# Attention with centred weights: in the first group, the means and the centring of the next group's weights one step later

## The reference

```python
x = x + tanh(g_xattn) * xattn(_layernorm(x), ctx, ...)
x = x + tanh(g_ffn)   * moe(_layernorm(x), ...)
# xattn, 16 query heads, 8 key heads, head size 128
q  = _ln(fp8_linear(ln_out, wq,  q_in_scale));   k = _ln(fp8_linear(ln_out, wk, k_in_scale))
v  = fp8_linear(ln_out, wv, v_in_scale)          # self attention:  core = gqa(q, k, v)
qx = _ln(fp8_linear(ln_out, wqx, qx_in_scale))
kx, vx = split(ctx @ w_kv_x.T); kx = _ln(kx)     # cross attention: xout = gqa(qx, kx, vx)
out = (div_clamp_fp8(cat(core, xout), proj_smooth) @ wproj.T) * scale
# moe: 8 experts, top 2, silu(x @ Wg) * (x @ Wu) @ Wd, weighted sum
# _ln(y) subtracts the mean of each head's 128 outputs and divides by their deviation
```

## Time and profile before

| | |
|---|---|
| median of 3 runs | 1162.47 us |
| the profiled execution: its time, its span | 1163.21 us, 1161.2 us |
| PE busy | 1088.4 us, 94% of the span |
| DVE busy | 816.1 us, 70% |
| ACT busy | 697.0 us, 60% |
| POOL busy | 494.0 us, 43% |
| mean granted TensorE clock | 0.974 |
| DMA, mean over the span | 92 GB/s |

### The profile page before, as it was taken

The page is one execution under the profiler, slowest core; times in us unless marked ns, Lnnn a source line. Parts: engine busy times, 40 slices in busy tenths (PEclk is TensorE's granted clock), DMA queues, the critical chain, the costliest instruction groups (busy, mean ns, idle before and its releaser), DMA issues. The chain is left out here.

```text
span 1161.2 us, 19646 instructions
## 1 busy us (share of the span) xinstructions
PE 1088.4 (94%) x5662; PEld 891.7 (77%) x5662; DVE 816.1 (70%) x1692; ACT 697.0 (60%) x2015; POOL 494.0 (43%) x571
## 2 busy tenths in 40 slices
PE   3499999999999999999999999998999869999996
PEld 2377878888888878888888888886888747777785
DVE  7989997887887797777788777777554785565000
ACT  7557878757887865788876665673231323444332
POOL 4154454445554445444535455452000125565432
PEclk8799999999999999999999999999999879999998
DMA  7231111114111125111112311111954347674220
GB/s 254 68 113 35 35 50 46 45 48 185 44 45 35 35 62 189 35 44 53 39 41 80 115 42 38 43 36 69 336 174 163 127 137 216 176 237 111 51 45 0
DMA packets 52820, 107.40 MB, mean 92 GB/s; under 512 B 6064, under 2 KB 27056, under 8 KB 51184
## 3 DMA queue, kind: packets, MB, share of 16 engines
q1 hardware_dynamic: 48016, 97.00, 25.6%
q0 software_dynamic: 4704, 9.18, 3.5%
HBM read 91.48 MB, written 16.52 MB: 93 GB/s over the span
## 5 line engine op out<-in xcount | busy, mean ns | idle before, releaser
L523 POOL TENSOR_TENSOR rs<-va,mhalf 125x2 f32<-125x2 f32 (+1 forms) x180 | 204.9, 1139 | 14.2 <-POOL va L516 0.2
L529 POOL TENSOR_TENSOR c_lo<-c_raw,c_hi 128x500 fp32r<-128x500 f32 x96 | 125.0, 1303 | 190.2 <-ACT c_hi L581 190.2
L796 PE MATMUL bank<-w_hi,c_hi 128*125 128x512 f32 x384 | 166.0, 432 | 9.9 <-POOL c_lo L529 9.9
L796 PE MATMUL bank<-w_hi,c_lo 128*125 128x512 f32 x384 | 151.8, 395 | 0.0
L796 PE MATMUL bank<-w_lo,c_hi 128*125 128x512 f32 x384 | 151.7, 395 | 0.0
L516 POOL TENSOR_TENSOR va<-ss,epst 125x2 f32<-125x2 f32 (+1 forms) x180 | 48.3, 269 | 199.6 <-DVE ss L1077 121.0
L770 PE MATMUL bank<-w_hi,xqs 128*128 128x512 f32 (+2 forms) x464 | 110.2, 359 | 16.1 <-DVE xqs L1069 10.1
L770 PE MATMUL bank<-w_lo,xqs 128*128 128x512 f32 (+2 forms) x464 | 100.8, 339 | 0.1
L660 ACT ACTIVATE work<-bank,nmax 112x375 f32<-112x375 f32 x128 | 73.6, 585 | 41.9 <-DVE nmax L1106 41.7
L840 PE MATMUL bank<-kxT,qxT 128*112 128x375 f32 x256 | 96.9, 480 | 0.0
L796 PEld LDWEIGHTS bank<-w_hi,c_hi 128*125 128x125 f32 x384 | 71.7, 187 | 28.3 <-issue 10.2
(11 more groups left out here) (265 smaller groups left out, 2813.1 us busy)
## 6 DMA issues: line engine op xcount, KB each, us to landing
c_raw<-in_ctxT SPq DMA_DIRECT2D x96, 250.0 KB, 2.7
shared<-in_w_in SPq DMA_DIRECT2D x13, 1024.0 KB, 8.5
shared<-in_wproj SPq DMA_DIRECT2D x32, 256.0 KB, 4.1
raw_g<-in_Wg SPq DMA_DIRECT2D x8, 1024.0 KB, 6.5
raw_u<-in_Wu SPq DMA_DIRECT2D x8, 1024.0 KB, 6.6
raw_d<-in_Wd SPq DMA_DIRECT2D x8, 1024.0 KB, 5.6
cat_scratch<-results SPq DMA_DIRECT2D x32, 224.0 KB, 2.0
shared<-cat_scratch SPq DMA_DIRECT2D x2, 1792.0 KB, 9.2
```

The source lines that it names most:

```text
L523: pool.tensor_tensor(rs[0:rows, lo:hi], va[0:rows, lo:hi], mhalf[0:rows, lo:hi], ALU.pow).then_inc(rs_done, 1)
L529: pool.tensor_tensor(flat(c_lo[:, k, :, :]), flat(c_raw[:, k, :, :]), flat(c_hi[:, k, :, :]).bitcast(F32), ALU.subtract).then_inc(cl_done, 1)
L796: m = pe.matmul(bank[0:CT, :], a[:, ch, k, :], w[:, k, CKX:CV], start=(i == 0), stop=(i == 3 * KB - 1))
```

## The change

In the first group alone, block k is summed in step k + 2 instead of k + 1 and centred in step k + 3 instead of k + 2. The last block is therefore centred in step (0, 6), which is also the "queries" step; since `w_high(g, 0)` needs all blocks, it is moved there from before `take(s, 4)` to after the last part of the centring. In the other groups nothing changes.

```diff
+def centred_from(gp):
+    return 3 if gp == 0 else 2
@@ passes
-                k = u - 2 if 2 <= u < 2 + KB else None
+                k = u - centred_from(gp) if 0 <= u - centred_from(gp) < KB else None
@@ ACT, step
             if k is not None: weights.centre(act, g, k, 0)
-            if change == "queries": w_high(g, 0, change)
+            if change == "queries" and k is None: w_high(g, 0, change)
             if A: take(s, 4)
             if k is not None: weights.centre(act, g, k, 1)
             if k is not None: weights.centre(act, g, k, 2)
+            if change == "queries" and k is not None: w_high(g, 0, change)
             if change == "queries": w_high(g, 1, change)
@@ DVE, step
-            if change is None and g is not None and s[1] <= KB: weights.means(v, g, s[1] - 1)
+            if g is not None and change is None and 0 <= s[1] + 1 - centred_from(s[0]) < KB:
+                weights.means(v, g, s[1] + 1 - centred_from(s[0]))
```

## The result

The change made the kernel a little slower. Twenty runs each: 1167.23 us median against 1164.02 us, 3.2 us apart; ratio of the changed kernel to the kernel before 1.0031, 95% interval 1.0021 to 1.0042. In time the ratio is +3.6 us, from 2.4 to 4.9. The direction and the mechanism were as forecast; the forecast of +2.4 us was too small, and the windows of the steps tell where. One of the twelve runs of experiment seven, 1844.84 us at a mean granted clock of 0.556, stands apart from all others and is left out of the ratio given there.

The account below looks back on a forecast made before the run. PE was taken to bound group 1 and DVE the first group's steps 2 to 4; -1.4 + 2.8 + 1.0 = +2.4 us on the median 1162.47 gave 1164.9 us, own range 1163.5 to 1166.5, wide range 1160.3 to 1168.3.

Parts of the forecast that it names:

- the net loss: At the step change, (0,6) with (0,7): PE's stall less what it gives back, plus the clock; 2.6 to 4.9 us.
- The gain at (0,2): PE's step (0,2): without the sums DVE is no longer late, so -1.4 us, at the lower end 1.0 gained.
- rival B: Steps (0,2) to (0,5): early start persists, all at 23.83 us; 1161.7 us, or 1157.8 with the stall hidden; chance 0.12.
- ACT's centring in (0,6): ACT's queue: 4.84 us more work makes `turned(t, 0)` late by about 3.65 us and stalls PE 3.4 us.
- Rival A: Step (0,6): the stall is hidden by more ACT slack or an existing wait; only -1.4 stays, 1161.1 us; chance 0.15.
- The clock: PE behind the new pause: granted clock falls to half speed, costing +1.0 us, between 0 and 1.7.
- What the stall gives back: Step (0,7): DVE and ACT work on during the stall, so old PE waits mostly vanish; 0.6 us, ends 0.2 and 0.8.
- the link from `max_self` to the two waits: Step (0,7): `max_self`, 0.67 us late, comes on time, so PE's waits of 0.28 and 0.38 us behind it mostly go.
- Rival C: ACT's lateness reaches (1,0), where PE waits again with a second lowered stretch; +5.9 us, 1168.4 us; chance 0.10.
- the two pauses in the earlier trace: PE pauses: 1.81 us left the clock at 1.0, 2.42 us was followed by 3.42 us at 0.5; evidence for +1.0.

Follow-up runs that it names:

- experiment seven: Kernel before the change with only DVE's order of rounding in the first group altered; (0,2) to (0,7) 143.07 us, ratio to the kernel before 0.9988.
- run two: Changed kernel without the thirteen centring instructions in (0,6), `w_high(g, 0)` back ahead of `take(s, 4)`; (0,2) to (0,7) 142.64 us.
- run four: Kernel before the change with DVE's sums and their scaling left out in the first group; steps (0,2) to (0,5) each run at 23.8 us.
- run one: Changed kernel with DVE's sums back where they stood before, only ACT's centring one step later; (0,2) to (0,7) 149.06 us.
- run six: Changed kernel with both `w_high` copies behind `turned(t, 0)` and DVE's `w_low` parts later; (0,2) to (0,7) 144.06 us, ratio to the kernel before 0.9991.
- run three: Changed kernel with twelve added 512-column matmuls on PE ahead of `project(s, 2)` in (0,7); (0,7) 23.77 us against 25.15, one timed run 1167.39 us.
- run five: Changed kernel with `w_high(g, 1)` moved to (0,7) behind `turned(t, 3)`, DVE's first half of `w_low(g, 1)` behind `rounded`; (0,2) to (0,7) 146.38 us.

## Why the prediction was right, and by how much it was short

*The number.* 1167.23 us lies in the wide range (1160.3 to 1168.3), but above the forecast's own (1163.5 to 1166.5). 1.55 us of its distance from 1164.9 come from the base: twenty runs of the kernel before have a median of 1164.02, the three that I started from 1162.47. Two narrower bounds were passed as well: (0,6) with (0,7) take 49.14 us where 46.9 to 48.6 stood, and the net loss there is 5.04 where 2.6 to 4.9 stood. And twenty runs of each did tell 0.3% from no change, which I had thought impossible under 0.5%.

*The gain at (0,2): right.* Forecast -1.4, measured -1.41 in the window, -1.42 in run two. That DVE is the bound there through sums and rounding together, that the lateness is not a backlog handed on (rival B), and that (0,3) to (0,5) would keep their lengths: shown by the unchanged windows and by run four. One reading was loose: of the three short waits for DVE in a step like (0,2), the middle one, at the first `turn_cross`, has ACT's `kxT` (L636) as its releaser, 0.29 us. It is gone in the changed kernel too, and run one, where only ACT was relieved, gained nothing.

*ACT's centring in (0,6): right, a little short.* The step-by-step count gave a pause of 3.4 us with `turned(t, 0)` as releaser. Measured are 3.54 us of idle time and PE 3.69 us later at that place; run two shows that it goes with the thirteen instructions, run six that the pause is gone, with the centring in place, once the copies queued behind it are moved. Rival A is out.

*The clock: right in kind, mis-sized.* I took +1.0 between 0 and 1.7. The fall came, and PE lost 1.4 us: 5.15 - 3.69 = 1.46 us while the clock was down, and run three, where it stayed up, is 1.38 us shorter in the step. The part that I had hoped would overlap the pause did not: the stretch began 0.15 us before PE went on.

*What the stall gives back: mis-sized, the largest single error.* I took 0.6 of 0.67 and 0.38 us of old waits. PE's lateness was 5.15 us behind the slow matmuls and 5.03 at the end of the step: 0.1 given back. The step that failed is the link from `max_self` to the two waits. `max_self` is on time now, as forecast (it waits 2.94 us for PE and starts 0.04 us behind the end of the scores instead of 0.67). But DVE then waits for PE's cross scores in `max_cross`, and `norm_self` (L1100, now L1107) starts 3.38 us behind the end of the scores instead of 3.50: of the 0.67 only 0.12 came through. The old waits were not made by `max_self`: already before, the second `norm_cross` ran beside POOL's `c_lo` and took 1.21 us instead of 0.41, just ahead of the 0.38 us wait. Now the first one does, PE's 0.40 us wait stands at the first `turn_cross`, and the one at the second is gone. The meeting moved by one place.

This is read from rows; no run moved that meeting alone. Before the change, DVE and POOL:

```profile
220.91 0.41 DVE L1113 TENSOR_SCALAR work<-work,linv 112x375 f32<-112x375 f32 x1
...
221.43 1.21 DVE L1113 TENSOR_SCALAR work<-work,linv 112x375 f32<-112x375 f32 x1
```

```profile
221.14 1.29 POOL L529 TENSOR_TENSOR c_lo<-c_raw,c_hi 128x500 fp32r<-128x500 f32 x1 [5.10 <-ACT c_hi L581]
```

And after it:

```profile
222.14 1.18 DVE L1113 TENSOR_REDUCE nmax<-bank 112x1 f32<-112x375 f32 x2 [0.23 <-PE bank L847]
...
225.37 1.22 DVE L1120 TENSOR_SCALAR work<-work,linv 112x375 f32<-112x375 f32 x1
```

```profile
225.09 1.28 POOL L535 TENSOR_TENSOR c_lo<-c_raw,c_hi 128x500 fp32r<-128x500 f32 x1 [5.62 <-ACT c_hi L587]
```

The sum with the measured terms is -1.4 + 3.7 + 1.4 - 0.1 = +3.6 against the forecast's -1.4 + 3.4 + 1.0 - 0.6 = +2.4, and the timed ratio agrees with the first. Rival C, a second wait in group 1, did not come: (1,0) takes 24.03 us after the change and 24.02 before.

The changed kernel's profiled span is 7.4 us longer, not 3.6. 0.9 us of the rest lie before (0,2) and 1.3 between the last `turn_self` and the projection (801.40 to 812.94, in the earlier trace rows 796.85 to 807.07), where that execution has one lowered stretch more; the last section tells why I take this for chance. What is left, 1.5 us, stands behind the start of the projection.

## What to carry to other kernels

Before work is moved to a later step, list what is queued behind its new place on the same in-order engine, and add the whole of it up to the first instruction that the bounding engine waits for: here 4.8 us of harmless work stood ahead of one small copy out of PSUM, and cost 3.7 us. Put such releasing copies ahead of bulk work whose consumer is far away. And where an engine is the bound in some steps only, taking work from it pays only in the steps where it falls under the others; a delay of one step frees one step, not all.

## What the runs showed of the hardware beyond that

Pauses of PE of the same length were followed by a lowered clock in some executions and not in others. At the end of the attention all eleven profiled executions have a pause of 1.81 us and one of 2.42 us. Behind the first the clock fell in five (the changed kernel and runs one, three, four and seven) and stayed up in the other six, the kernel before among them; behind the second it fell in seven. The stretch of the changed kernel behind the pause of 1.81 us:

```profile
802.41:805.82 3.41, 3.41 (x10) 2.07 (x10) 2.19 (x5) 0.66 (x2) 0.00 (x0) 0.50 0.00 0
```

So the two pauses in the earlier trace rows were weaker evidence than I used them for: the clock at 1.0 behind 1.81 us was one outcome of two. Behind the pause of 3.54 us it fell both times it was profiled, and behind 1.74 us in run five it did not. The Trainium skill, "TensorE: Matmul & The Clock Gate", section "Part 1: The HAM clock gate", says that the gate's timing runs freely and doesn't start with the kernel, so that the same kernel differs from run to run; the eleven executions, each of another kernel but with the same two pauses, agree with it. A lowered stretch cost 1.3 to 1.5 us in the places measured above. The runs' clocks point the same way: among 23 timed runs of the kernel before, those with a mean granted clock of 0.974 or more took 1161.59 to 1163.78 us, and the three with 0.970 or less 1168.37 to 1168.62. So this is probably a part of why runs of one kernel spread over 7 us; the stretches of those runs were not traced.

The second is the meeting of DVE and POOL, seen both ways: DVE's bf16 subtraction (L213) beside `c_lo` takes 1.66 instead of 0.62 us, and POOL's `c_lo` beside DVE's `w_low` 2.84 instead of 1.25. The Trainium skill, "SBUF — State Buffer", section "SBUF: two separate sides", says that the two engines share a pair of ports as a lock, which whichever starts first holds for a whole instruction; on DVE's side that goes for some instructions, among them those with two inputs in SBUF. The rows of run five agree (both instructions have two inputs there): `c_lo` was started 0.55 us after `w_low`, and ends 1.1 us after it, as if it had run nearly whole once the other was done.
